# Attention on one Trainium2 core: softmax denominators summed over four key steps, with an accumulating transfer, and one narrow group of products per two steps

## The reference

```python
h = _sln(hidden, w, ...)
qkv = (h @ Wqkv.T + bqkv).reshape(B, N, num_heads, hd, 3)
energy = jnp.einsum('bhqd,bhkd->bhqk', q, k)
att = jax.nn.softmax(energy, axis=-1) / D ** 0.5
out = jnp.einsum('bhqk,bhkd->bhqd', att, v)
out = out @ Wp.T + bp
h1 = out + hidden
return _sln(h1, w, ...) + h1
```

## Time and profile before

| | |
|---|---|
| three runs, us | 1978.65, 1978.87, 1980.02 |
| the profiled execution, us | 1979.28 |
| its span, first to last instruction, us | 1977.3 |
| mean granted TensorE clock | 0.975 |
| attention stage, us from the span's start | 952 to 1857.5 |

### The profile page before, as it was taken

One profiled execution on the slowest core, in us unless ns is written; L12 is line 12 of the kernel. 1 busy time (PEld: TensorE's weight loads), 2 busy tenths in 40 slices (PEclk: granted clock), 3 DMA queues, 4 the chain that ended last, 5 costly groups with the idle time before them and its releaser, 6 DMA issues. The chain is left out here.

```text
span 1977.3 us, 28224 instructions
## 1 busy us (share of the span) xinstructions
PE 1898.2 (96%) x10520; PEld 1242.1 (63%) x10520; DVE 1212.2 (61%) x1510; ACT 808.7 (41%) x1373; POOL 1146.5 (58%) x589
## 2 busy tenths in 40 slices
PE   6599999999998999998999999999999999999996
PEld 1478888888886888885455555555555555554484
DVE  3556555555646544445766666666666666664199
ACT  1322123122212222211466666666666666666400
POOL 0574565466445121122377777777777777777555
PEclk9799999999999999998799999999999999999998
DMA  7301010100113464566344323444442234414194
GB/s 242 124 1 54 34 53 21 53 32 21 53 38 138 151 216 166 192 199 191 87 98 103 72 78 90 103 97 109 108 103 71 78 92 103 97 35 177 64 398 156
DMA packets 117687, 212.46 MB, mean 107 GB/s; under 512 B 18598, under 2 KB 36134, under 8 KB 117576
## 3 DMA queue, kind: packets, MB, share of 16 engines
q1 hardware_dynamic: 93980, 190.60, 32.5%
q10 hardware_dynamic: 23408, 20.37, 3.2%
q0 software_dynamic: 192, 0.05, 0.0%
HBM read 134.40 MB, written 75.80 MB: 106 GB/s over the span
## 5 line engine op out<-in xcount | busy, mean ns | idle before, releaser
L1371 DVE TENSOR_REDUCE at_mrow<-banks 128x1 f32<-128x1024 f32 x512 | 604.2, 1217 | 272.0 <-PE banks L1204 271.9
L1349 ACT ACTIVATE at_probs<-banks 128x512 f32<-128x512 f32 x1024 | 557.2, 597 | 326.4 <-PE banks L1220 325.3
L1468 POOL TENSOR_TENSOR at_pair<-at_probs 128x2048 f32<-128x2048 f32 x127 | 581.2, 4576 | 173.2 <-ACT at_probs L1349 173.2
L1220 PE MATMUL banks<-early_qs,early_ks 98*128 98x512 f32 x1024 | 441.9, 434 | 5.5 <-ACT at_probs L1349 5.5
L1204 PE MATMUL banks<-early_ks,early_qs 96*128 96x512 f32 x1024 | 377.5, 413 | 6.7 <-PEq L754 3.6
L1220 PEld LDWEIGHTS banks<-early_qs,early_ks 98*128 98x128 f32 x1024 | 191.8, 188 | 211.8 <-ACT at_probs L1349 108.9
L1232 PE MATMUL banks<-at_probs,at_v 128*32 128x512 f32 x2048 | 273.6, 606 | 0.9 <-ACT at_probs L1349 0.9
L1204 PEld LDWEIGHTS banks<-early_ks,early_qs 96*128 96x128 f32 x1024 | 198.6, 197 | 45.4 <-DVE at_mrow L1371 18.8
L67 PE MATMUL banks<-l_ht,l_weights 128*128 128x512 f32 x768 | 178.9, 392 | 5.6 <-ACT l_gt L574 5.6
L67 PE MATMUL banks<-qk_nt,l_weights 128*128 128x512 f32 x768 | 177.1, 392 | 3.0 <-ACT qk_gt L889 3.0
L67 PE MATMUL banks<-l_weights,l_hf 128*128 128x512 f32 x768 | 177.3, 390 | 0.0
(11 more groups left out here) (120 smaller groups left out, 1987.9 us busy)
## 6 DMA issues: line engine op xcount, KB each, us to landing
qk_scratch<-qk_out SPq DMA_DIRECT2D x64, 512.0 KB, 2.8
early_ks<-qk_scratch SPq DMA_DIRECT2D x48, 512.0 KB, 7.0
early_qs<-qk_scratch SPq DMA_DIRECT2D x96, 256.0 KB, 11.6
attn_scratch<-at_out SPq DMA_DIRECT2D x32, 512.0 KB, 2.6
o_a<-attn_scratch SPq DMA_DIRECT2D x32, 512.0 KB, 13.0
v_scratch<-qk_v ACTq DMA_DIRECT2D x32, 256.0 KB, 2.4
at_v<-v_scratch SPq DMA_DIRECT2D x16, 512.0 KB, 14.1
o_x<-x_scratch SPq DMA_DIRECT2D x8, 1024.0 KB, 15.6
```

Source lines behind the costliest of these rows:

```text
L1220: pe.matmul(et[j % 2][:], ks[0:98, slot, j, (i % KC) * P:(i % KC + 1) * P], qs[0:98, slot, i // KC, j, :], start=True, stop=True).then_inc ...
L1349: nc.scalar.activation(probs[:, i % 4, j, :], et[j % 2][:], ACT.Exp).then_inc(exp_done, 1)
L1371: nc.vector.tensor_reduce(mrow[:, half, u:u + 1], e_ps[u % 2], AX.XY, ALU.max).then_inc(max_done, 1)
L1468: nc.gpsimd.tensor_tensor(psum2[:, pair % 2], probs[:, a], probs[:, a + 1], ALU.add).then_inc(pair_ready, 1)
```

## The change

Five things change, all in `attention_stage` and the stack loads.

Denominators: GpSimd adds pairs as before, but the first pair of every four steps ("quad") goes to one of two tiles of `sums`, and the second to the third tile, a scratch. An accumulating transfer from GpSimd's queue then adds the scratch to the first tile, and TensorE multiplies by ones once per quad.

Order on TensorE: 16 wide products in one run per pair of steps (`FRONT`), then both steps' `av`, with `den` between or behind them in every second pair. The lag from a pair to its denominator products is set by `LAG`.

Banks: three for energies and three for maxima, used in turn; each maximum is over 512 keys, and the two halves of the keys are joined after two transposes.

Small operations of GpSimd: the product is written over `av_sb`, and `round_off` becomes a copy. They move in the order of the group.

Loads: keys at the group's start, each half of the queries later, v last.

```diff
-def load_stack(eng, sh, qs, ks, g, slot):
+def load_stack_keys(eng, sh, ks, g, slot):
+def load_stack_queries(eng, sh, qs, g, slot, half):
...
-        LEAD = 13
-        SWITCH = STEPS - LEAD
-        TURN = (SWITCH + KC + 1, SWITCH + 1)
+        LEAD = 6
+        SWITCH = PAIRS - LEAD
+        TURN = (SWITCH + PAIRS // 2, SWITCH)
+        QUADS = PAIRS // 2
+        LAG = 3
+        SPAN = PAIRS // QH
+        FRONT = ("M", "E") * 5 + ("E", "M") * 3
...
-        psum2 = sb("at_pair", [P, 2, HG, CH])
+        sums = sb("at_sums", [P, 3, HG, CH])
...
-        et = sh.ps[0:2]
-        e_ps = [sh.psum[:, 2:4], sh.psum[:, 4:6]]
+        et, em = sh.ps[0:3], sh.ps[3:6]
...
             def group(g, slot, nth=None, first=False, load=True, with_next=True):
+                if not first and load:
+
+                    sp.wait_ge(av_done, STEPS * g)
+                    load_keys(g + 2, (slot + 2) % RING)
...
                 if not first:
+                    spread_den(g - 1, 1)
                     store(g - 1, 0)
-                    spread_den(g - 1, 1)
                 place_neg(g, slot, 1)
                 if not first:
                     widen_rden(g - 1, 1)
+                if not first and load:
+                    load_queries(g + 2, (slot + 2) % RING, 0)
...
+                spread_den(g, 0)
+                if not first:
                     store(g - 1, 1)
-                spread_den(g, 0)
+                if not first and load:
+                    load_queries(g + 2, (slot + 2) % RING, 1)
                 if with_next:
                     place_neg(g + 1, (slot + 1) % RING, 0)
                 widen_rden(g, 0)
+                if not first and load:
+                    load_v(g + 2, (slot + 2) % RING)
...
+            def max_unit(g, slot, half, u, keys):
+                n, j, c = number(g, half, u, keys), u // TT, u % TT
+                if n >= 3:
+
+                    pe.wait_ge(max_done, n - 2)
+                pe.matmul(em[n % 3][:], qs[0:96, slot, half, j, c * P:(c + 1) * P],
...
+                for keys in range(2):
+                    last = pe.transpose(den_ps[0:UNITS, keys * P:(keys + 1) * P], mrow[:, half, keys], sh.ident[:])
+                last.then_inc(mrow_turned, 1)
...
+                if n >= 3:
+
+                    pe.wait_ge(exp_done, n - 2)
+                pe.matmul(et[n % 3][:], ks[0:98, slot, j, (i % KC) * P:(i % KC + 1) * P],
...
+            def den(g, quad):
+                q = QUADS * g + quad
+                pe.wait_ge(quad_ready, 16 * (q + 1))
...
+                for part in range(PARTS):
                     cols = slice(DC * part, DC * (part + 1))
                     for j in range(HG):
...
+                        last = pe.matmul(den_ps[HD * j:HD * (j + 1), cols], ones_col[:], sums[:, q % 2, j, cols],
...
+            def den_before(g, p):
+
+                if p >= LAG:
+                    den(g, (p - LAG) // 2)
+                elif g > 0:
+                    den(g - 1, QUADS + (p - LAG) // 2)
...
+                    for kind in FRONT:
+                        if kind == "E":
+                            energies(g, slot, 2 * p + e // HG, e % HG)
+                            e += 1
+                        else:
+                            for product in islice(products, 1):
                                 max_unit(*product)
+                    if p == TURN[1]:
+                        turn_max(g, 1)
+                    if with_next and p == TURN[0]:
+                        turn_max(g + 1, 0)
+                    av(g, slot, 2 * p)
+                    if p % SPAN == 1:
+                        den_before(g, p)
+                    av(g, slot, 2 * p + 1)
+                    if p % SPAN == SPAN - 1:
+                        den_before(g, p)
...
+                    if i % KC == KC - 1:
+                        take_av(g, i // KC)
+                    if i == 3 and not first:
                         take_den(g - 1, 1)
-                    if i == KC + KC // 2 - 1:
+                    if i == KC + 3:
                         take_den(g, 0)
...
+                nc.vector.tensor_reduce(mrow[:, half, keys, u:u + 1], em[n % 3][:], AX.X, ALU.max).then_inc(max_done, 1)
...
+                nc.vector.tensor_reduce(joined, den_ps[0:UNITS, 0:2 * P].rearrange("u (k c) -> u c k", c=P), AX.X, ALU.max).then_inc(maxima_joined, 1)
...
-                nc.gpsimd.tensor_tensor(out[:, half, HI], av_sb[:, half], rden[:, half], ALU.mult).then_inc(out_hi, 1)
+                nc.gpsimd.tensor_copy(out[:, half, HI], av_sb[:, half]).then_inc(out_hi, 1)
...
+                    quad, second = divmod(PAIRS * g + pair, 2)
                     pool.wait_ge(exp_done, HG * (STEPS * g + 2 * pair + 2))
-                    if not (first and pair < 2):
-
-                        pool.wait_ge(den_done, PAIRS * g + pair - 1)
...
+                    if second and quad >= 1:
+
+                        pool.wait_ge(quad_ready, 16 * quad)
+                    if not second and quad >= 2:
+
+                        pool.wait_ge(den_done, quad - 1)
+                    into, a = sums[:, 2 if second else quad % 2], 2 * pair % 4
+                    nc.gpsimd.tensor_tensor(into, probs[:, a], probs[:, a + 1], ALU.add).then_inc(pair_ready, 1)
+                    if second:
+                        pool.wait_ge(pair_ready, PAIRS * g + pair + 1)
+                        pool.dma_start(sums[:, quad % 2].rearrange("p j c -> p (j c)"), into.rearrange("p j c -> p (j c)"),
+                                       accum_op=ALU.add).then_inc(quad_ready, 16)
```

More of the change, by code:

```diff
@@ L1 @@
 from contextlib import ExitStack
+from itertools import islice
 import concourse.bass as bass
@@ L1092, in groups, with units_of_pair, number @@
             group(15, 2, load=False, with_next=False)
-        def units_of_step(g, slot, i, with_next):
-            if i >= SWITCH and not with_next:
+        def units_of_pair(g, slot, p, with_next):
+            if p >= SWITCH and not with_next:
                 return []
[L1098 to L1102, removed]
+            whose, at = (g + 1, (slot + 1) % RING) if p >= SWITCH else (g, slot)
+            n = 4 * ((p - SWITCH) % PAIRS)
+            return [(whose, at, (n + a) // UNITS, (n + a) % UNITS, keys) for a in range(4) for keys in range(2)]
+        def number(g, half, u, keys):
+            return 2 * (UNITS * (QH * g + half) + u) + keys
+        FIRST_UNITS = 4 * LEAD
         block = ctx.enter_context(nc.Block())
@@ L1160, in group @@
                         sp.wait_ge(out_free[half], 16 * (KT + 1))
[L1161 to L1169, removed]
+                    load_attended(sp, sh, 0)
                 if not first:
+                    spread_den(g - 1, 1)
                     store(g - 1, 0)
-                    spread_den(g - 1, 1)
                 place_neg(g, slot, 1)
@@ L1180, in group @@
                 widen_rden(g, 0)
+                if not first and load:
+                    load_v(g + 2, (slot + 2) % RING)
+                if not with_next:
+                    load_residual(sp, sh, 1)
+                    for b in range(2):
+                        load_style(sp, sh, b)
             load_v(0, RING - 1)
@@ L1234, in av @@
                 last.then_inc(av_done, 1)
[L1236 to L1245, removed]
+            def den(g, quad):
+                q = QUADS * g + quad
+                pe.wait_ge(quad_ready, 16 * (q + 1))
+                n = quad % (QUADS // QH)
+                if n == 0:
+                    if q > 0:
+                        pe.wait_ge(den_taken, q // (QUADS // QH))
+                    pe.wait_ge(negt_taken, min(halves(g, quad * QH // QUADS) + 1, QH * G))
+                for part in range(PARTS):
@@ new lines, in group @@
+                for p in range(PAIRS):
+                    if p % SPAN == 0:
+                        pe.wait_ge(negm_loaded, 32 * halves(g, p // SPAN))
+                    if with_next and p == SWITCH:
+                        pe.wait_ge(stack_loaded[nxt], LOADS * (nth + 1))
+                    products = iter(units_of_pair(g, slot, p, with_next))
+                    e = 0
+                    for kind in FRONT:
[4 more added lines that the diff above has]
+                            for product in islice(products, 1):
+                                max_unit(*product)
+                    if p == TURN[1]:
[8 more added lines that the diff above has]
+                        den_before(g, p)
@@ L1310, in _ @@
             groups(pe, group)
-            av(G - 1, RING - 1, STEPS - 1)
-            den(G - 1, PAIRS - 2, range(PARTS))
-            for n in (2, 3):
+            pe.wait_ge(pair_ready, PAIRS * G - 1)
+            tiles = [sums[:, (QUADS * G - 1) % 2], probs[:, 2], probs[:, 3]]
+            for tile in tiles:
                 for j in range(HG):
-                    last = pe.matmul(den_ps[HD * j:HD * (j + 1), :], ones_col[:], probs[:, n, j, :], start=False, stop=n == 3)
```

(1 more changed line is left out.)

163 lines of the change are left out of this document (57 added, 106 removed).

## The result

The changed kernel takes 2028.1 us (median of four runs, 2026.4 to 2035.3) against 1979.4: 1.025 times as long, with an interval of 1.023 to 1.028. The forecast was 1927 and the range ended at 2010, so both the direction and the range were wrong. The profiled execution, 2035.3 us, is the longest of the four; its span is 2033.2.

The account below looks back on a forecast made before the run. TensorE was taken to bound the attention stage, busy 899.7 of 905.5 us. From 1979.3 us, -73 (stream less waits), +5 and -2 (small parts) and +18 (company of loads) gave 1927; range 1890 to 2010.

Parts of the forecast that it names:

- TensorE's stream: TensorE's products in the attention stage: fewer wide/narrow changes and half the denominator products save 0.77 us a pair of steps.
- the waits within the run: TensorE's 16 wide products wait for VectorE's maxima, taken at 0.65 us each: 0.20 us lost a pair.
- The transfer by itself: GpSimd's accumulating transfer without company: landing in 7.3 us, free of charge up to 8.4, so nothing added.
- T: Time from the end of GpSimd's second add to the accumulating transfer's semaphore: 7.3 us taken, bounds 4.2 to 9.2.
- Company is dearer: Accumulating transfers meeting SyncE's loads and stores land later: 1.1 us a group, +18 us in all, ends 0 and 74.
- small parts: Small items on the path: an extra transpose per half, +5 us; single maxima at the start, -2 us; others nothing.
- The even sharing: Transfer and other traffic split the DMA engines evenly: up to 1.8 and 5.0 us added in two quads.
- Rival (3): Offset rows for the next group's first half land 1 to 3 us late: 30 us more, 1957; chance 0.06.
- Rival (1): The accumulating transfer sets the pace at GpSimd's second add if T averages over 9.56 us: slower, 2007 to 2071; chance 0.28.

Follow-up runs that it names:

- e1b: Changed kernel without the accumulating transfer, so denominators hold only the first pair of every four steps: 1896.0 us (0.958 of before).
- e4: Changed kernel, transfer kept, but stack loads of groups 3 to 15 fetch 16 columns a head (v: one chunk): 1924.8 us (0.973).
- e8b: Changed kernel with the transfer's bytes moved from a fixed tile to an unread one, so no engine waits for the data: 1989.9 us (1.005).
- e2: Changed kernel with SyncE's second query loads issued behind the offset rows and inverse denominators instead of ahead: 2027.7 us (1.025).
- e3: Changed kernel with all ten stack loads back at the group's start: 2028.8 us (1.025).
- e5: Changed kernel with the transfer copying the second sum over the first instead of adding it, all waits kept: 1949.7 us (0.985).

## Why the prediction was wrong

- **TensorE's stream and the waits within the run** were right and a little too careful: 73 - 5 + 2 = 70 us were forecast, e1b shows 83. A pair without a denominator takes 5.97 us there and one with it 6.84, mean 6.41, where the sum had 6.50. A maximum took 0.68 us and not 0.65, so that the wait should have been longer; yet the run of 16 took 4.12 us for the 3.99 + 0.20 of the sum, a wait of 0.13. So the wait was mis-sized, by little.
- **The transfer by itself** was sized well: T was put at 7.3 us, and measured in e4 are 7.2 from the issue, some 7.5 from the end of the add. It was called free up to 8.4, and nothing was forecast; e4 still shows 29 us, with stores and the many small packets beside it. Which of these it is stays open. The estimate of 6.8 us from the Trainium skill ("DMA: Bandwidth & Descriptors", Anatomy of one DMA, and "Collectives: The Full Stack", The bandwidth ceiling) was short by about half a microsecond, and its halved rate for an add is near the measured factor of 1.84.
- **The step that failed is the one that begins "Company is dearer"**: +18 us, 1.1 a group, with an upper end of 74. Measured are 103 us, 6.4 a group, for the loads. With it the sum reads: stream, waits and small parts -83 for -70, the transfer beside small loads +29 for 0, company of the loads +103 for +18, together +49 for -52. The even sharing was worked out for the transfer's landing alone, over by 0.7 and 3.9 us in two quads. In the sum it was not worked out for the other side, SyncE's small transfers: the offset rows landed in 6.0 us where they had needed 2.1, and TensorE waited; the inverse denominators took 4.5 to HBM where they had needed 1.4, their load back stands behind that, and GpSimd waited.
- **Rival (3)** named that place rightly (the offset rows of the next group's first half) and priced it at 30 us with a chance of 0.06. e8b shows that with the transfer's traffic alone this path costs 94: by its trace the idle time at the offset rows, nearly all of it at group starts (3.5 us and 4.1 where the half within the group has 0.5), is about two thirds, and the lower clock the rest by estimate. (These 94 and the 103 of e4 are two different cuts through the same 132 and do not add.) The clock was not in the rival's price: in the changed kernel it falls to the lower level after the 3.5 us of idling and makes the next products about half as fast for 3 us. GpSimd's waits for the inverse denominators held up nothing of TensorE in e8b. In the changed kernel they also shift the next transfer, and TensorE is idle for 29.4 us at the ones products beside 48.9 at the offset rows.
- **Rival (1)**, the transfer as the pace, had the right sign, and its condition was not met: T was 8.3 us in the median, 11.6 at most in 1000 to 1800, and had to average over 9.56. But in e2 and e3, with the rows out of the way, the same loss is paid at the very place it names, by one late transfer a group: in three arrangements of the loads the wait changes its owner and the time stays at 2028. The rule of the Trainium skill's page "DMA: Bandwidth & Descriptors" (Queues, rings and completion order), that each engine takes the queues in turn, spoke for a price on both sides; the trace agrees in kind, with loads and transfer both slower when they meet (medians: keys 8.3 us in e1b and 10.0 in the changed kernel, queries 4.8 and 7.9, the transfer 7.2 in e4 and 8.0). The even split itself was not measured.

The forecast's miss is thus the company of the loads, worked out for one side and too low there. Still open are what the 29 us of e4 are made of, and how far the share of each queue goes by packets and how far by bytes: e4 took bytes away and kept the packets, and no run did the reverse.

## What to carry to other kernels

A transfer that lands in time by its own duration is not free: work out what else lands later while it runs, small dependent transfers first, since each has a place in a chain. When the same loss shows up under another wait after each reordering, look at what meets what, and gate one stream on the other's semaphore before giving up either; and use a costly device only where the other traffic leaves room (two transfers a group beat all four by 94 us here, and by 27 where the loads of the four were gated).

## What was not expected of the hardware

- An accumulating transfer of 1 MB takes the DMA engines 1.84 times as long per byte as a copy (e5), and GpSimd 0.87 us to issue, where 8 KB took 0.56.
- SyncE's issues get slower too when GpSimd's queue is busy: the three query loads behind the store took 3.8 to 4.3 us to issue in every group of the changed kernel (1100 to 1750 us), where the same three took 1.8 in nearly all groups of e1b.
- A GpSimd operation of 128x512 with one input (the new `round_off`, at 1320.95) takes 0.60 us undisturbed, about half of the 1.28 that the product with two inputs takes.
